# VectorE takes the third row maximum ahead of a tile's end in every unit of a cross-attention kernel

## The reference: what is computed

```python
Q, K, V = x @ Wq.T + bq, ctx @ Wk.T + bk, ctx @ Wv.T + bv     # split into 16 heads
scores = einsum('bhqd,bhkd->bhqk', Q, K) / sqrt(32)
scores = where(mask == 0, -1e9, scores)
attn = softmax(scores)                                        # over the keys
out = (attn @ V, heads joined) @ Wo.T + bo + x
return layernorm(out) * ln_g + ln_b
```

## Time and profile before

| | |
|---|---|
| median of three runs | 1701.11 us (1695.54 to 1701.28) |
| the profiled execution's own time | 1703.89 us |
| its span, first to last instruction | 1701.8 us |
| TensorE busy | 1649.6 us, 97% |
| VectorE busy | 1153.7 us, 68% |
| ScalarE busy | 1346.9 us, 79% |
| GpSimd busy | 1303.6 us, 77% |
| mean granted TensorE clock | 0.985 of full |

### The profile page before, as it was taken

The page is one execution under the profiler, slowest core; times in us unless marked ns, Lnnn a source line. Parts: engine busy times, 40 slices in busy tenths (PEclk is TensorE's granted clock), DMA queues, the critical chain, the costliest instruction groups (busy, mean ns, idle before and its releaser), DMA issues.

```text
span 1701.8 us, 24832 instructions
## 1 busy us (share of the span) xinstructions
PE 1649.6 (97%) x7742; PEld 982.3 (58%) x7742; DVE 1153.7 (68%) x2835; ACT 1346.9 (79%) x1540; POOL 1303.6 (77%) x845
## 2 busy tenths in 40 slices
PE   6889999999999999999999999999999999999987
PEld 4546566565656656565665656656565665656532
DVE  7566766767676676766667676676776667677653
ACT  4388798888879788887878879887887888878673
POOL 7085787879778788878869778787877878887674
PEclk9999999999999999999999999999999999999987
DMA  7877585776767677577667668677676767756501
GB/s 251 257 211 202 161 243 175 206 200 199 204 196 217 188 203 216 169 218 208 192 179 205 203 173 241 179 203 200 191 204 204 211 185 204 217 162 187 162 8 68
DMA packets 180194, 327.51 MB, mean 192 GB/s; under 512 B 37344, under 2 KB 37344, under 8 KB 180064
## 3 DMA queue, kind: packets, MB, share of 16 engines
q1 hardware_dynamic: 180064, 325.93, 66.7%
HBM read 236.72 MB, written 89.13 MB: 191 GB/s over the span
## 4 chain that ended last, share of the span: by engine, by line
PE 89%; DMA 3%; DVE 3%; POOL 2%; issue 1%; ACT 1%; SPq 1%; POOLq 0%; DVEq 0%; ACTq 0%
PE proj_bank L969 43%; PE ctx_bank L893 14%; PE ring L862 13%; PE exp_banks L877 13%; PE ring L913 3%; DMA stack_scratch<-qk_lo 3%; PE ring L922 1%; POOL total L460 1%; DVE ring L691 1%; DVE qk_lo L719 1%; POOL c_lo L445 0%; POOL total L468 0%; PE exp_banks L987 0%; ACT qk_hi L598 0%; POOL x_lo L445 0%
## 5 line engine op out<-in xcount | busy, mean ns | idle before, releaser
L691 DVE CUSTOM_DVE_ANT_0 ring<-ring,bias 128x512 f32<-128x512 f32 x1024 | 691.2, 710 | 340.4 <-PE ring L862 340.3
L578 ACT ACTIVATE probs<-exp_banks 128x1024 f32<-128x1024 f32 x512 | 523.9, 1023 | 249.9 <-PE exp_banks L877 249.6
L552 ACT CAST exp_banks<-biasT 128x1024 f32<-128x1024 bf16 x512 | 520.7, 1017 | 25.2 <-DVE biasT L761 1.6
L877 PE MATMUL exp_banks<-q_stack,k_stack 98*128 98x512 f32 x1024 | 375.8, 449 | 3.7 <-ACT exp_banks L552 3.7
L862 PE MATMUL ring<-k_stack,q_stack 96*128 96x512 f32 x1024 | 333.3, 403 | 14.9 <-DVE maxes L691 11.9
L468 POOL TENSOR_TENSOR total<-total,probs 128x1024 f32<-128x1024 f32 x126 | 297.3, 2380 | 9.0
L460 POOL TENSOR_TENSOR total<-total,probs 128x2048 f32<-128x2048 f32 x63 | 290.0, 4603 | 10.5 <-ACT probs L578 3.9
L460 POOL TENSOR_TENSOR total<-probs 128x2048 f32<-128x2048 f32 x63 | 290.2, 4606 | 0.0
L893 PE MATMUL ctx_bank<-probs,v 128*32 128x512 f32 x2048 | 277.5, 614 | 0.7 <-DVE ctxT L752 0.7
L877 PEld LDWEIGHTS exp_banks<-q_stack,k_stack 98*128 98x128 f32 x1024 | 194.6, 191 | 107.0 <-issue 66.4
L475 POOL CAST max_parts<-maxes 128x16 fp32r<-128x16 f32 x64 | 12.5, 196 | 303.0 <-DVE maxes L691 303.0
(11 more groups left out here) (105 smaller groups left out, 1920.1 us busy)
## 6 DMA issues: line engine op xcount, KB each, us to landing
w_tile<-w_scratch SPq DMA_DIRECT2D x120, 512.0 KB, 4.6
k_stack<-stack_scratch SPq DMA_DIRECT2D x192, 256.0 KB, 5.4
q_stack<-stack_scratch SPq DMA_DIRECT2D x192, 256.0 KB, 7.1
stack_scratch<-qk_hi SPq DMA_DIRECT2D x128, 256.0 KB, 2.2
stack_scratch<-qk_lo SPq DMA_DIRECT2D x128, 256.0 KB, 2.5
raw<-cT_dram SPq DMA_DIRECT2D x64, 256.0 KB, 5.0
raw<-xT_dram SPq DMA_DIRECT2D x64, 256.0 KB, 4.9
raw<-mask_dram SPq DMA_DIRECT2D x64, 256.0 KB, 4.5
```

The lines of the kernel that those rows point to most:

```text
L552: nc.scalar.copy(exp_banks[:, 2 - 2 * wave:4 - 2 * wave, :], biasT[:, kc:kc + 1, :].to_broadcast([P, 2, L])).then_inc(seeded, 1)
L578: nc.scalar.activation(probs[:, u % PS, 2 - 2 * wave:4 - 2 * wave, :], exp_banks[:, 2 - 2 * wave:4 - 2 * wave, :], ACT.Exp).then_inc(exps, 1)
L691: nc.vector.tensor_tensor_reduce(out=ring[:, n % 2], in0=ring[:, n % 2], in1=bias[:, c], scale=1.0, scalar=LOWEST, op0=ALU.subtract, op1=A ...
L877: mm = nc.tensor.matmul(exp_banks[:, h], k_stack[0:3 * D + 2, at, kc * P:(kc + 1) * P], q_stack[0:3 * D + 2, at, :], start=False, stop=Tru ...
```

## The change

In every unit VectorE now takes maximum 2 ahead of `finish_tile`. The condition is gone. Nothing is added and nothing is removed from any engine's list; on VectorE two items change places where the condition was false.

```diff
                 tile = PLAN.tile(y - 1)
-                ring_wanted = PLAN.sums(y) or PLAN.mask(y)
                 if tile and tile[0] == "O":
                     bias_output(tile)
-                if ring_wanted:
-                    row_max(y, 2)
+                row_max(y, 2)
                 if tile:
                     finish_tile(tile)
-                if not ring_wanted:
-                    row_max(y, 2)
                 row_max(y, 3)
```

## The result

The changed kernel takes 1729.72 us (median of four runs, 1726.9 to 1734.71) against 1700.16 us for the kernel before (four runs). The ratio is 1.0182, with a 95% interval of 1.0152 to 1.0213. The forecast was 1729 us and slower, by the mechanism "forecast as summed". The profiled execution took 1734.71 us, the slowest of the four; its span is 1732.4 us. After the edit the lines behind line 779 stand 4 lower: 858 is the 862 of before, 965 the 969.

A forecast was written before the change was run, and what follows sets the result against it. TensorE was taken as the bound, busy 1649.6 of 1701.8 us. Waits of 18.0 (K and Q), 7.8 (O) and 2.0 us (place 9) sum to 27.8; on the median of 1701.11 us that gave 1729 us, range 1718 to 1737.

The forecast's parts named there:

- forecast as summed: Main case: late tile ends make TensorE wait before projections, 27.8 us in all, 1729 us; chance 0.91.
- K and Q tiles: Units at places 2, 6, 7, 10: `qk_lo` ends later, so the next projection load waits 0.30 us, 60 times, 18.0 us.
- S + 1.55: Start of the next projection's weight load before the change, S being the start of scores 2 and 3; predicted S + 1.85 after.
- the 1.15 us: VectorE's idle time ahead of `qk_lo`; claimed no help, since score 2 and `qk_hi` come within 0.02 us of each other.
- O tiles: Units at places 3 and 5: maximum 2 delays line 715, so the projection load waits 0.26 us, 30 times, 7.8 us.
- place 9: Unit behind the sums, projection load already at S + 1.72; claimed to move to S + 1.85, 0.13 us, 15 times, 2.0 us.
- Nothing given back: Claim that later work does not make up the holes, since each delays all streams equally; a sequence takes 1.85 us more.
- The sum: Waits on TensorE over all changed places: 18.0 + 7.8 + 2.0 = 27.8 us.
- two units of the filling: Units y = -6 and -4 before y = 0 also change order; either sign, at most about 0.6 us each, counted as nothing.
- Late stores: SyncE's store of `qk_lo` goes about 0.62 us later and may hold ScalarE; counted 0, range -2 to +5 us.
- The clock: Rival: the new small holes bring a granted-clock dip in each of 15 sequences, 26 us longer still, 1755 us; chance 0.04.

The follow-up runs named there:

- both maxima first: Changed against the kernel before: in the units that changed order, maximum 2 and maximum 3 both go ahead of the tile's end; 1791.36 us, ratio 1.0526.
- both uniform ones: Against the kernel before: maximum 2 ahead of the tile's end in every unit, 1729.72 us; the tile's end ahead of maximum 2 in every unit, 1740.6 us.

## Why the prediction was right

**K and Q tiles.** Predicted 0.30 us at places 2, 6, 7, 10; measured 0.30, 0.29, 0.30, 0.29. The step that carried it was to take the new order's times from a unit that had it already and the due time from the unit to be changed. That S + 1.55 is a due time and not chance is shown by moving the end by twice as much (the load follows one for one) and by moving score 2 away (the hole goes).

**The idle time of VectorE was no cover.** I had argued that score 2 and `qk_hi` become available at the same moment, so that the 1.15 us could take nothing in. With score 2 0.47 us sooner the same maximum does fit, and most of the loss comes back. That shows it from the other side.

**O tiles and place 9.** Predicted 0.26 and 0.13 us; measured 0.25 (place 3), 0.23 (place 5) and 0.12.

**Nothing given back.** 1.81 us a sequence for 1.85 expected. The undisturbed sequences account for 27 of the 29.6 us. The sum was 27.8, which is 1.0164 of the medians, inside the interval of the ratio. That 1729 us met the 1729.72 to less than 1 us is in part luck: the four runs of the kernel after alone lie 7.8 us apart.

**What the sum did not hold.** In the profiled execution the first sequence takes 6.8 us more (108.03 against 101.27, from its first maximum to the first of the next sequence). The changed places 2, 6, 7 and 9 in it explain 1.0 us at most, and two units of the filling 0.6 us each by the prediction's bound. Before, then after, then with K and Q alone:

```profile
34.90:136.20 101.30, 84.82 (x357) 50.89 (x357) 58.61 (x155) 59.80 (x72) 47.07 (x32) 0.93 0.80 234
```
```profile
34.90:142.90 108.00, 89.29 (x356) 54.10 (x356) 58.52 (x154) 60.19 (x72) 49.04 (x32) 0.89 0.75 220
```
```profile
35.10:136.40 101.30, 87.55 (x357) 51.84 (x356) 58.52 (x154) 58.00 (x70) 46.00 (x32) 0.90 0.78 230
```

After the change the granted clock is lower there (0.89 for 0.93), and one score stands still for 2.98 us where it was 1.54. The kernel with K and Q alone changed tells whether the new order did it: no O tile ends before the second sequence, so in the first it has the same order of work on every engine as the kernel after, and it took 101.27 us. With the O tiles alone changed, which leaves the first sequence as it was before, it took 99.74. So starts of one and the same order lie up to 6.8 us apart, and this start doesn't show an effect of the change. What makes a start slow, no run tells. In the ten traces of this study the first sequence took from 99.47 to 109.06 us.

**Late stores.** I had let the range hold them. ScalarE waited for one 15 times instead of 10, and those at place 13 stopped TensorE at most 1.4 us, for 1.73 before. What the first fifteen units at place 13 took above 6.12 us is 4.6 us in all, before 6.1: no clear difference in the sum.

**The clock** did not follow the holes: with both maxima first, seven holes of 0.8 to 0.9 us in every 107 us left the granted clock at 1.00 for 1400 us, and so did the seven of 0.12 to 0.30 us in the kernel after. The Trainium skill's page "TensorE: Matmul & The Clock Gate" (section "A second HAM failure mode: psum-queue depth-cycling") speaks for that rival. These traces disagree with carrying its rule over to holes of this size and spacing.

## What to carry to other kernels

When two instructions of an engine with spare time change places, ask of each who waits for it and when it is due there: the difference between its end and that due time is all that the swap may use, and idle time ahead of it counts only if the other instruction's input is there by then. Where an engine is full, read the new order's times from a place of the same trace that already has it, and count start to start, not the idle time in the brackets. An order by cases is best checked by running each case alone and the opposite everywhere; here the order by cases beat both uniform ones, by 30 and 39 us, and the gain that was left lay in when the input came.
